# Token mixer, attention and thirty feed-forward passes: who adds 0.01 tanh, and who adds the variance's constant

## The chip, the cores and the metric

The kernel runs on one core of one Trainium2 chip. The metric is the time of one execution on the device in microseconds. The kernel before has a median of 1579.58 us over three runs (1578.74 to 1583.05).

## The reference

Frames of 75 joints go through three graph layers and a mean (the tokens), text is appended, one attention layer is added, and then a feed-forward part. The change lies in that last part, which goes thirty times over a matrix `x` of 64 x 96 rows of 64 numbers:

```
def step(h, _):
    h = h + 0.01 * jnp.tanh(h)
    h = h * jax.nn.sigmoid(h)
    h = _layernorm(h, ln_w, ln_b)      # (h - mean) * rsqrt(var + 1e-5) * ln_w + ln_b
    h = jnp.einsum('bsc,dc->bsd', h, W) + b
    return (h, None)
x, _ = jax.lax.scan(step, layernorm(h), None, length=30)
out = h + x
```

## The kernel before

The last stage (`feed_forward`, from L1178) cuts the 6144 rows into six chunks. A chunk is a tile of 128 partitions x 512 numbers, eight rows of 64 on a partition. Each chunk owns one bank of PSUM (`ps[:, c]`), in which its `x` stays for all thirty passes; two more banks take the transposes.

A *step* is one chunk of one pass: 180 steps. All engines go through the steps in the same order (`steps`, L1225), each as an in-order queue, and are held together by semaphores alone. The first twelve steps are written out, then a loop of 28 turns with six steps in each, then five closing steps. In step `s` the engines work on chunks of different age: tanh and the addition on step `s`, silu and statistics on `s-1`, the scaling and the transposes on `s-3`, the copy of the transposed tile on `s-4`, the matrix on `s-5`. A chunk thus comes back to its own bank six steps later.

For one chunk the work is:

- ScalarE: `th = tanh(x)` (L1313).
- the addition `x + 0.01 th` in PSUM: TensorE for even chunks, as a product of `th` with a diagonal matrix `pct` that is accumulated into the bank (L1345), VectorE for odd chunks (L1402). In the opening pass VectorE does all six, in SBUF (L1398). Two semaphores `y_ready` count the two kinds; the waiting side counts halves (`half(lag)`).
- ScalarE: `g = silu(.)` from PSUM to SBUF (L1323).
- VectorE: four `bn_stats`, each over a pair of rows interleaved, which leave mean and summed squares of the deviations (64 times the variance) of every row (L1360); then, behind a wait for its own statistics, the sum of that and `D * EPS` into `var` (L1363).
- GpSimd: `rs = var ** -0.5` as a two-input power, 128 x 8 (L1296).
- VectorE: the scaling `gn = g * rs` (L1409). The mean isn't subtracted here: the weights were centred beforehand.
- TensorE transposes four 128 x 128 squares (L1353), ScalarE copies them to SBUF (L1330), TensorE writes the bias into the bank and accumulates the matrix (L1338, L1340).

VectorE's order within a step is: addition (if it is its turn), scaling of `s-3`, statistics of `s-1`. So the scaling of one chunk comes two steps after its statistics, with one scaling and one set of statistics between. `var`, `rs`, the pairs of the statistics and `gn` have two buffers each. GpSimd's power of step `n` waits for `var` of `n` and for the scaling of `n-2`.

Of the kernel before, what the change touches and what calls it, by code (L numbers as in the profile page):

```python
# [22 lines left out]
ALU = mybir.AluOpType  # L23
# [4 lines left out]
P = 128  # L28
# [3 lines left out]
D = 64  # L32
# [1145 lines left out]
def feed_forward(nc, ctx, ps, h2, h2_loaded, ident, wf, pct, ones, brow, out):  # L1178
# [8 lines left out]
    def sb(name, shape, dt=F32):  # L1187
        return ctx.enter_context(nc.sbuf_tensor(name, shape, dt))
# [11 lines left out]
    var, var0 = (sb(f"var64_{i}", [P, n, CR]) for i, n in enumerate((2, CH)))  # L1200
    rs, rs0 = (sb(f"rs_{i}", [P, n, CR]) for i, n in enumerate((2, CH)))
    expo = sb("expo", [P, CR])
    warm = sb("warm", [P, 1])

    bn0 = sem("bn_done0")
# [19 lines left out]
    def steps(eng, body, before=None):  # L1225

        for s in range(2 * CH):
            if before and s < CH:
                before(s)
            body(s, s % CH, lambda lag, s=s: s - lag >= 0, lambda lag, s=s: (s - lag) // 2 - CH // 2)  # L1230
        with eng.Fori(1, ITERS - 1) as it:
            for c in range(CH):
                body(it * CH + CH + c, c, lambda lag: True, lambda lag, c=c: it * (CH // 2) + (c - lag) // 2)
        for s in range(N, N + LAG):
            body(s, s - N, lambda lag, s=s: 0 <= s - lag < N, lambda lag, s=s: (s - lag) // 2 - CH // 2)

    def opening(n):

        return isinstance(n, int) and n < CH
# [5 lines left out]
    def squares(pairs, b):  # L1245
        return pairs[:, b].rearrange("p j (i k) -> p (j i) k", i=2)[:, :, 2]
# [28 lines left out]
    def prepare_pool(pool, t):  # L1275

        if t == 10:
            pool.memset(expo[:], -0.5).then_inc(expo_made, 1)
            pool.wait_ge(expo_made, 1)
        if t in STATS_AT:  # L1280
            pool_root(pool, STATS_AT.index(t))
        if t in CENTRE_AT:
            pool_centre(pool, CENTRE_AT.index(t))

    def gpsimd(pool):
        def before(s):
            if s in LATE_STATS_AT:
                pool_root(pool, EARLY + LATE_STATS_AT.index(s))

        def body(s, c, on, half):  # L1290
            if on(1):
                n, b = s - 1, (c - 1) % 2
                pool.wait_ge(var_done, n + 1)
                if late(n, 2):
                    pool.wait_ge(gn_done, n - 1)
                nc.gpsimd.tensor_tensor(rs[:, b, :], var[:, b, :], expo[:], ALU.pow).then_inc(rs_done, 1)  # L1296
        steps(pool, body, before)

    def scalar(act):

        nc.scalar.activation(warm[:], ident[:, 0:1], ACT.Silu)

        def body(s, c, on, half):
            if on(0):
                if opening(s):
                    act.wait_ge(x0_ready, s + 1)
                else:
                    act.wait_ge(x_ready, s - CH + 1)
                if late(s, CH + 2):
                    act.wait_ge(y_ready[c % 2], half(2) + 1)  # L1310
                elif late(s, 2):
                    act.wait_ge(y0_made, s - 1)
                nc.scalar.activation(th[:, c % 2, :], x0[:, c, :] if opening(s) else ps[:, c, :],  # L1313
                                     ACT.Tanh).then_inc(th_done, 1)
            if on(1):
                n, cn = s - 1, (c - 1) % CH
                if opening(n):
                    act.wait_ge(y0_made, n + 1)
                else:
                    act.wait_ge(y_ready[cn % 2], half(1) + 1)  # L1320
                if late(n, NG):
                    act.wait_ge(gn_done, n - NG + 1)
                nc.scalar.activation(g_[:, cn % NG].rearrange("p r d -> p (r d)"), x0[:, cn, :] if opening(n) else ps[:, cn, :],  # L1323
                                     ACT.Silu).then_inc(g_done, 1)
            if on(4):
                n, b = s - 4, c % 2
                act.wait_ge(gT_ready, n + 1)
                if late(n, 2):
                    act.wait_ge(x_ready, n - 1)
                nc.scalar.activation(gT[:, b, :], ps[:, TB + b, :], ACT.Identity).then_inc(gT_done, 1)  # L1330
        steps(act, body)

    def tensor(pe):
        def body(s, c, on, half):
            if on(5):
                n, cn, b = s - 5, (c - 5) % CH, (c - 5) % 2
                pe.wait_ge(gT_done, n + 1)
                nc.tensor.matmul(ps[:, cn, :], ones[:], brow[:], start=True, stop=False, skip_group_check=True)  # L1338
                for j in range(CP):
                    last = nc.tensor.matmul(ps[:, cn, j * P:(j + 1) * P], gT[:, b, j * P:(j + 1) * P], wf,  # L1340
                                            start=False, stop=(j == CP - 1), skip_group_check=True)
                last.then_inc(x_ready, 1)
            if on(0) and c % 2 == 0 and not opening(s):
                pe.wait_ge(th_done, s + 1)
                nc.tensor.matmul(ps[:, c, :], pct[:], th[:, c % 2, :], start=False, stop=True,  # L1345
                                 skip_group_check=True).then_inc(y_ready[0], 1)
            if on(3):
                n, b = s - 3, (c - 3) % 2
                pe.wait_ge(gn_done, n + 1)
                if late(n, 2):  # L1350
                    pe.wait_ge(gT_done, n - 1)
                for j in range(CP):
                    last = nc.tensor.transpose(ps[:, TB + b, j * P:(j + 1) * P], gn[:, b, j, :], ident[:])  # L1353
                last.then_inc(gT_ready, 1)
        steps(pe, body)

    def statistics(dve, src, pairs, var, b, n, bns, made):

        for j in range(CP):
            last = v_.bn_stats(pairs[:, b, j, :], src[:, 2 * j:2 * j + 2, :].rearrange("p i d -> p d i"))  # L1360
        last.then_inc(bns, 1)
        dve.wait_ge(bns, n + 1)
        v_.tensor_scalar(var[:, b, :], squares(pairs, b), D * EPS, None, ALU.add).then_inc(made, 1)  # L1363

    def first_statistics(dve, c):
        dve.wait_ge(h2_loaded, (c + 1) * 16)
        statistics(dve, rows(c), bs0, var0, c, c, bn0, var0_done)

    def first_scale(dve, c):
        x = x0[:, c, :].rearrange("p (r d) -> p r d", d=D)  # L1370
# [12 lines left out]
    def vector(dve):  # L1383
        def before(s):
            if s in LATE_STATS_AT:
                c = EARLY + LATE_STATS_AT.index(s)
                first_statistics(dve, c)
                v_.tensor_tensor(x0[:, c, :].rearrange("p (r d) -> p r d", d=D), rows(c),
                                 spread(means(bs0, c), P, CR), ALU.subtract).then_inc(centred[1], 1)
            if s in LATE_SCALE_AT:  # L1390
                c = EARLY + LATE_SCALE_AT.index(s)
                dve.wait_ge(centred[1], c - EARLY + 1)
                first_scale(dve, c)

        def body(s, c, on, half):
            if on(0) and opening(s):
                dve.wait_ge(th_done, s + 1)
                v_.scalar_tensor_tensor(x0[:, c, :], th[:, c % 2, :], 0.01, x0[:, c, :],  # L1398
                                        ALU.mult, ALU.add).then_inc(y0_made, 1)
            elif on(0) and c % 2 == 1:  # L1400
                dve.wait_ge(th_done, s + 1)
                v_.scalar_tensor_tensor(ps[:, c, :], th[:, c % 2, :], 0.01, ps[:, c, :],  # L1402
                                        ALU.mult, ALU.add).then_inc(y_ready[1], 1)
            if on(3):
                n, cn, b = s - 3, (c - 3) % CH, (c - 3) % 2
                dve.wait_ge(rs_done, n + 1)
                if late(n, 2):
                    dve.wait_ge(gT_ready, n - 1)
                v_.tensor_tensor(gn[:, b].rearrange("p j (i d) -> p (j i) d", i=2), g_[:, cn % NG],  # L1409
                                 spread(rs[:, b, :], P, CR), ALU.mult).then_inc(gn_done, 1)  # L1410
            if on(1):
                n, cn, b = s - 1, (c - 1) % CH, (c - 1) % 2
                dve.wait_ge(g_done, n + 1)
                if late(n, 2):
                    dve.wait_ge(rs_done, n - 1)
                statistics(dve, g_[:, cn % NG], bs, var, b, n, bn_done, var_done)
        steps(dve, body, before)
        for c in range(CH):
            dve.wait_ge(x_ready, N - CH + c + 1)
            v_.tensor_tensor(h2[:, c, :], h2[:, c, :], ps[:, c, :], ALU.add).then_inc(out_done, 1)  # L1420
# [45 lines left out]
```

## Time and profile before

| | |
|---|---|
| median of three runs | 1579.58 us |
| the profiled execution's own time | 1579.94 us |
| its span, first to last instruction | 1578.1 us |
| TensorE (PE) busy | 1505.3 us, 95% |
| VectorE (DVE) busy | 1368.2 us, 87% |
| GpSimd (POOL) busy | 1240.5 us, 79% |
| ScalarE (ACT) busy | 1154.8 us, 73% |

These shares are means over the whole span. The tokens take the first 1100 us or so, the attention about the next 100, and the last stage runs from 1208 us to the end. To judge a change in that stage one reads stretches of it, a turn of the loop for instance, and the order of single instructions in the timeline. An instruction that an engine holds in its queue for a semaphore isn't busy time; one that has started and can't get its data is.

### The profile page before, as it was taken

The numbers are of one execution on the slowest core, as the hardware profiler recorded it, in microseconds if no ns is written. First come the engines' busy times: TensorE is split into PE (matmuls) and PEld (weight loads), VectorE is DVE, ScalarE is ACT, GpSimd is POOL, SyncE is SP. The second block draws the span as 40 slices with busy tenths as digits, with TensorE's granted clock in tenths as the row PEclk, the third lists the DMA queues.
The fourth block names the chain that finished last, engine by engine and source line by source line (L and its number), as shares of the span: only waits on it lengthen the run. The fifth ranks groups of instructions, "written<-read, shape, count | busy, mean of one in ns | idle before, by whom it ended". The sixth has DMA issues, their size and how long they took to land. (4 is left out here: it accounts for less than half of the span.)

```text
span 1578.1 us, 64590 instructions
## 1 busy us (share of the span) xinstructions
PE 1505.3 (95%) x22398; PEld 1162.8 (74%) x22398; DVE 1368.2 (87%) x3354; ACT 1154.8 (73%) x2706; POOL 1240.5 (79%) x1295
## 2 busy tenths in 40 slices
PE   8599999999999999999999999999495999999998
PEld 8477777777777777777777777776484888888887
DVE  7388888888888888888888888888578999999998
ACT  3477787777777777778777777776054888787876
POOL 2288888888888888888888888888167888888887
PEclk9999999999999999999999999999696999999999
DMA  5300000000000000000000000000111000000001
GB/s 116 100 9 7 7 7 7 7 7 7 7 7 7 7 7 7 7 7 7 7 7 7 7 7 7 7 7 6 19 46 36 1 0 0 0 0 0 0 0 40
DMA packets 21670, 21.66 MB, mean 14 GB/s; under 512 B 12254, under 2 KB 19342, under 8 KB 21271
## 3 DMA queue, kind: packets, MB, share of 16 engines
q1 hardware_dynamic: 18554, 19.07, 4.5%
q0 software_dynamic: 1120, 1.44, 0.4%
q10 hardware_dynamic: 1972, 0.86, 0.3%
q8 instruction: 13, 0.21, 0.1%
q14 instruction: 11, 0.09, 0.0%
HBM read 14.43 MB, written 6.92 MB: 14 GB/s over the span
## 5 line engine op out<-in xcount | busy, mean ns | idle before, releaser
L703 DVE SCALAR_TENSOR_TENSOR y<-ps,negb,abar 128x375 f32<-128x375 f32 x820 | 459.4, 602 | 95.2 <-PE ps L603 95.1
L657 POOL TENSOR_TENSOR y0lo<-y_whole,y0hi 128x384 f16<-128x384 f32 x410 | 375.1, 915 | 165.5 <-ACT y_whole L631 152.3
L581 PE MATMUL ps<-AThi,y0hi 64*128 64x150 f16 (+1 forms) x4920 | 434.6, 217 | 3.4 <-POOL y0lo L657 3.4
L581 PE MATMUL ps<-AThi,y0lo 64*128 64x150 f16 (+1 forms) x4920 | 435.2, 215 | 0.0
L581 PE MATMUL ps<-ATlo,y0hi 64*128 64x150 f16 (+1 forms) x4920 | 434.9, 214 | 0.0
L666 POOL TENSOR_TENSOR y<-y 128x370 f32<-128x370 f32 x410 | 399.0, 973 | 2.0 <-DVE y L703 1.9
L629 ACT ACTIVATE y0hi<-ps 128x384 f16<-128x384 f32 x410 | 202.7, 494 | 234.4 <-POOL y0lo L657 220.5
L1296 POOL TENSOR_TENSOR rs<-var,expo 128x8 f32<-128x8 f32 x180 | 313.8, 1753 | 49.7 <-DVE var L1363 49.7
L603 PE MATMUL ps<-z_whole,W1s 128*128 128x375 f32 x820 | 313.7, 504 | 0.0
L638 ACT ACTIVATE z_whole<-ps 128x375 f32<-128x375 f32 x615 | 268.8, 493 | 1.4 <-PE ps L581 1.4
L581 PEld LDWEIGHTS ps<-ATlo,y0hi 64*128 64x128 f16 x4920 | 244.2, 96 | 0.0
L581 PEld LDWEIGHTS ps<-AThi,y0hi 64*128 64x128 f16 x4920 | 239.3, 94 | 4.3 <-POOL y0lo L657 3.7
L691 DVE SCALAR_TENSOR_TENSOR y0lo<-ps,y0hi 128x384 f16<-128x384 f32 x410 | 226.6, 553 | 18.0 <-ACT y0hi L629 17.6
L581 PEld LDWEIGHTS ps<-AThi,y0lo 64*128 64x128 f16 x4920 | 238.7, 94 | 0.0
L631 ACT ACTIVATE y_whole<-ps 128x384 f32<-128x384 f32 x410 | 209.7, 511 | 0.0
L630 ACT ACTIVATE y0hi<-ps 128x384 f16<-128x384 f32 x410 | 204.4, 498 | 0.0
L1340 PEld LDWEIGHTS ps<-w,gT 128*128 128x128 f32 x1440 | 189.9, 192 | 7.6
L603 PEld LDWEIGHTS ps<-z_whole,W1s 128*128 128x128 f32 x820 | 139.2, 189 | 73.1
L1340 PE MATMUL ps<-w,gT 128*128 128x128 f32 x1440 | 190.5, 275 | 0.0
L715 DVE TENSOR_REDUCE pooledT<-y 128x190 f32 (+3 forms) x410 | 182.5, 446 | 0.7 <-POOL y L666 0.7
L560 PEld LDWEIGHTS ps<-W0K,z_static 64*128 64x128 f16 x2460 | 73.6, 95 | 123.3 <-issue 119.5
L597 PE MATMUL ps<-z_whole,W1s 128*128 128x375 f32 x410 | 162.6, 478 | 0.0
(201 smaller groups left out, 2366.2 us busy)
## 6 DMA issues: line engine op xcount, KB each, us to landing
z_static<-z_rows SPq DMA_DIRECT2D x410, 18.0 KB
xs<-in_x_v SPq DMA_DIRECT2D x5, 720.7 KB, 8.6
z_rows<-zp SPq DMA_DIRECT2D x10, 240.0 KB
h_rows<-h SPq DMA_DIRECT2D x16, 96.0 KB, 1.9
h2r<-h_rows SPq DMA_DIRECT2D x6, 256.0 KB, 2.6
out<-h2r SPq DMA_DIRECT2D x6, 256.0 KB, 2.3
z_rows<-zp POOLq DMA_DIRECT2D x5, 240.0 KB, 3.0
h<-in_txt SPq DMA_DIRECT2D x1, 512.0 KB, 5.0
```

What stands on the lines that cost most here:

```text
L581: last = nc.tensor.matmul(ps[:, Z1B + 2 * p + j, f0 * V:f0 * V + w], y[rows, par, p, t * C:(t + 1) * C], a[rows, BAND0[t]:BAND0[t] + w], s ...
L603: nc.tensor.matmul(ps[:, Y1B[1][i], 0:GV], W1s[:], z1f[:, par, 1 + i, :], start=True, stop=True).then_inc(y1_ready[i], 1)
L629: nc.scalar.activation(y0hi[:, par, p, HC:2 * HC], ps[:, Y0B + 1, 0:HC], ACT.Relu).then_inc(y0hi_done, 1)
L630: nc.scalar.activation(y0hi[:, par, p, 0:HC], ps[:, Y0B, 0:HC], ACT.Relu).then_inc(y0hi_done, 1)
L631: nc.scalar.activation(y0f[:, p, :], ps[:, Y0B, 0:HC], ACT.Relu).then_inc(y0f_done, 1)
L638: nc.scalar.activation(z1f[:, par, 2 * p + i - 1, :], ps[:, Z1B + 2 * p + i, 0:GV], ACT.Identity).then_inc(z1f_done, 1)
L657: nc.gpsimd.tensor_tensor(y0lo[:, par, p, 0:HC], y0f[:, p, :], y0hi[:, par, p, 0:HC], ALU.subtract).then_inc(y0lo_by_pool, 1)
L666: nc.gpsimd.tensor_tensor(y[:, :, U1:2 * U1], y[:, :, U1:2 * U1], y[:, :, 0:U1], ALU.add).then_inc(halved, 1)
L691: nc.vector.scalar_tensor_tensor(y0lo[:, par, p, HC:2 * HC], ps[:, Y0B + 1, 0:HC], 0.0, y0hi[:, par, p, HC:2 * HC], ALU.max, ALU.subtract) ...
L703: nc.vector.scalar_tensor_tensor(y1[:, par, 2 * p + i].rearrange("p f v -> p (f v)"), ps[:, Y1B[p][i], 0:GV], negb1[:, 0:1], abar[:].rearr ...
L1296: nc.gpsimd.tensor_tensor(rs[:, b, :], var[:, b, :], expo[:], ALU.pow).then_inc(rs_done, 1)
L1340: last = nc.tensor.matmul(ps[:, cn, j * P:(j + 1) * P], gT[:, b, j * P:(j + 1) * P], wf, start=False, stop=(j == CP - 1), skip_group_check ...
```

## The change

TensorE adds 0.01 tanh in chunks 0 and 3 and VectorE in the other four (before: 0, 2, 4 and 1, 3, 5). The two counts of `y_ready` follow that; waits take a pair (pass, chunk) and not a half. The instruction L1363 on VectorE, with its wait, goes from the loop. In its place GpSimd adds a tile `eps64` that holds `D * EPS` to the statistics, two inputs of 128 x 8, into `var`. It waits for the statistics and for the power of the step before, and the power waits for this addition. The statistics ahead of the loop keep their instruction on VectorE.

```
+    eps64 = sb("eps64", [P, CR])
...
+    def added_by_tensor(c):
+        return c % 3 == 0
+
+    def wait_added(eng, place):
+        k, c = place
+        if added_by_tensor(c):
+            eng.wait_ge(y_ready[0], k * (CH // 3) + c // 3 + 1)
+        else:
+            eng.wait_ge(y_ready[1], k * (CH - CH // 3) + c - c // 3)
...
         if t == 10:
+            pool.memset(eps64[:], D * EPS)
...
                 n, b = s - 1, (c - 1) % 2
+                pool.wait_ge(bn_done, n + 1)
+                if late(n, 1):
+                    pool.wait_ge(rs_done, n)
+                nc.gpsimd.tensor_tensor(var[:, b, :], squares(bs, b), eps64[:], ALU.add).then_inc(var_done, 1)
                 pool.wait_ge(var_done, n + 1)
...
-                    act.wait_ge(y_ready[c % 2], half(2) + 1)
+                    wait_added(act, place(2))
...
-            if on(0) and c % 2 == 0 and not opening(s):
+            if on(0) and added_by_tensor(c) and not opening(s):
...
-        last.then_inc(bns, 1)
-        dve.wait_ge(bns, n + 1)
-        v_.tensor_scalar(var[:, b, :], squares(pairs, b), D * EPS, None, ALU.add).then_inc(made, 1)
+        last.then_inc(made, 1)
...
-            elif on(0) and c % 2 == 1:
+            elif on(0) and not added_by_tensor(c):
...
-                statistics(dve, g_[:, cn % NG], bs, var, b, n, bn_done, var_done)
+                statistics(g_[:, cn % NG], bs, b, bn_done)
```

## Rows read from the trace of the kernel before

**Rows 1.** Stretches: from:to, length, busy us (instructions) of each engine, TensorE's clock, DMA
```profile
1398.84:1410.85 12.01, 12.01 (x86) 10.00 (x85) 11.42 (x39) 9.62 (x19) 10.42 (x6) 1.00 0.00 0
...
1170.00:1180.00 10.00, 8.23 (x86) 7.50 (x84) 7.60 (x23) 5.06 (x15) 8.09 (x10) 1.00 0.28 76
```

**Rows 2.** Groups, whole run: line, operation, shapes, count | busy us, mean ns | idle before, releaser
```profile
L666 POOL TENSOR_TENSOR y<-y 128x370 f32<-128x370 f32 x410 | 399.0, 973 | 2.0 <-DVE y L703 1.9
...
L1296 POOL TENSOR_TENSOR rs<-var,expo 128x8 f32<-128x8 f32 x180 | 313.8, 1753 | 49.7 <-DVE var L1363 49.7
...
L1360 DVE BATCH_NORM_STATS2 bn_pairs<-g 128x6 f32<-128x128 f32 x720 | 158.1, 282 | 0.6 <-ACT g L1323 0.6
...
L1409 DVE TENSOR_TENSOR gn<-g,rs 128x512 f32<-128x512 f32 x180 | 123.9, 688 | 12.1 <-issue 10.4 <-POOL rs L1296 1.4
...
L669 POOL TENSOR_TENSOR y<-y 128x190 f32<-128x190 f32 x205 | 109.0, 532 | 16.1
...
L1048 POOL TENSOR_TENSOR hn<-hc,rstd 96x256 f32<-96x256 f32 x16 | 9.7, 609 | 9.4 <-PE ps L1104 8.0 <-POOL hc L1043 0.8
...
L1272 POOL TENSOR_TENSOR x<-h2r,bn_pairs 128x512 f32<-128x512 f32 x4 | 4.2, 1049 | 0.0
```

**Rows 3.** Chain that ended last, 1400 to 1410: start us, length us, what
```profile
1403.91 0.86 PE ps L1345 x2
...
1404.77 0.44 PE ps L1353 x4
...
1405.20 0.22 PE ps L1338
...
1405.42 0.89 PE ps L1340 x8
```

**Rows 4.** Timeline, 1400 to 1413: start us, length us, engine, line, operation [idle before]
```profile
1400.80 0.70 DVE L1402 SCALAR_TENSOR_TENSOR ps<-th,ps 128x512 f32<-128x512 f32 x1
...
1401.03 1.64 POOL L1296 TENSOR_TENSOR rs<-var,expo 128x8 f32<-128x8 f32 x1 [0.52 <-DVE var L1363]
...
1401.40 0.69 DVE L1409 TENSOR_TENSOR gn<-g,rs 128x512 f32<-128x512 f32 x1
...
1402.01 0.88 DVE L1360 BATCH_NORM_STATS2 bn_pairs<-g 128x6 f32<-128x128 f32 x4
...
1402.92 0.17 DVE L1363 TENSOR_SCALAR var<-bn_pairs 128x8 f32<-128x8 f32 x1
...
1403.00 0.69 DVE L1409 TENSOR_TENSOR gn<-g,rs 128x512 f32<-128x512 f32 x1
...
1405.22 0.69 DVE L1409 TENSOR_TENSOR gn<-g,rs 128x512 f32<-128x512 f32 x1
...
1406.82 0.69 DVE L1409 TENSOR_TENSOR gn<-g,rs 128x512 f32<-128x512 f32 x1
...
1411.19 0.69 DVE L1409 TENSOR_TENSOR gn<-g,rs 128x512 f32<-128x512 f32 x1 [0.38 <-issue]
```

**Rows 5.** Timeline of GpSimd alone, three short windows behind 1403
```profile
1403.25 1.94 POOL L1296 TENSOR_TENSOR rs<-var,expo 128x8 f32<-128x8 f32 x1 [0.58 <-DVE var L1363]
...
1403.25 3.54 POOL L1296 TENSOR_TENSOR rs<-var,expo 128x8 f32<-128x8 f32 x2 [0.58 <-DVE var L1363]
...
1406.99 2.01 POOL L1296 TENSOR_TENSOR rs<-var,expo 128x8 f32<-128x8 f32 x1 [0.21 <-DVE var L1363]
```

**Rows 6.** Timeline of GpSimd in the attention
```profile
1169.11 0.10 POOL L1278 MEMSET expo<- 128x8 f32 x1
...
1184.01 0.61 POOL L1043 TENSOR_TENSOR hc<-h,mean 96x256 f32<-96x256 f32 x1
...
1184.70 0.61 POOL L1048 TENSOR_TENSOR hn<-hc,rstd 96x256 f32<-96x256 f32 x1
```

More of the change, by code:

```diff
@@ L1229, in steps @@
                 before(s)
-            body(s, s % CH, lambda lag, s=s: s - lag >= 0, lambda lag, s=s: (s - lag) // 2 - CH // 2)
+            body(s, s % CH, lambda lag, s=s: s - lag >= 0, lambda lag, s=s: ((s - lag) // CH - 1, (s - lag) % CH))
         with eng.Fori(1, ITERS - 1) as it:
             for c in range(CH):
-                body(it * CH + CH + c, c, lambda lag: True, lambda lag, c=c: it * (CH // 2) + (c - lag) // 2)
+                body(it * CH + CH + c, c, lambda lag: True, lambda lag, c=c: (it + (c - lag) // CH, (c - lag) % CH))
         for s in range(N, N + LAG):
-            body(s, s - N, lambda lag, s=s: 0 <= s - lag < N, lambda lag, s=s: (s - lag) // 2 - CH // 2)
+            body(s, s - N, lambda lag, s=s: 0 <= s - lag < N, lambda lag, s=s: ((s - lag) // CH - 1, (s - lag) % CH))
+    def added_by_tensor(c):
[6 more added lines that the diff above has]
+            eng.wait_ge(y_ready[1], k * (CH - CH // 3) + c - c // 3)
     def opening(n):
@@ L1288, in before, with body @@
                 pool_root(pool, EARLY + LATE_STATS_AT.index(s))
-        def body(s, c, on, half):
+        def body(s, c, on, place):
             if on(1):
                 n, b = s - 1, (c - 1) % 2
+                pool.wait_ge(bn_done, n + 1)
+                if late(n, 1):
+                    pool.wait_ge(rs_done, n)
+                nc.gpsimd.tensor_tensor(var[:, b, :], squares(bs, b), eps64[:], ALU.add).then_inc(var_done, 1)
                 pool.wait_ge(var_done, n + 1)
@@ L1301, in scalar, with body @@
         nc.scalar.activation(warm[:], ident[:, 0:1], ACT.Silu)
-        def body(s, c, on, half):
+        def body(s, c, on, place):
             if on(0):
@@ L1319, in body @@
                 else:
-                    act.wait_ge(y_ready[cn % 2], half(1) + 1)
+                    wait_added(act, place(1))
                 if late(n, NG):
@@ L1333, in tensor, with body @@
     def tensor(pe):
-        def body(s, c, on, half):
+        def body(s, c, on, place):
             if on(5):
@@ L1355, in tensor, with statistics @@
         steps(pe, body)
-    def statistics(dve, src, pairs, var, b, n, bns, made):
+    def statistics(src, pairs, b, made):
         for j in range(CP):
             last = v_.bn_stats(pairs[:, b, j, :], src[:, 2 * j:2 * j + 2, :].rearrange("p i d -> p d i"))
-        last.then_inc(bns, 1)
-        dve.wait_ge(bns, n + 1)
-        v_.tensor_scalar(var[:, b, :], squares(pairs, b), D * EPS, None, ALU.add).then_inc(made, 1)
+        last.then_inc(made, 1)
     def first_statistics(dve, c):
         dve.wait_ge(h2_loaded, (c + 1) * 16)
-        statistics(dve, rows(c), bs0, var0, c, c, bn0, var0_done)
+        statistics(rows(c), bs0, c, bn0)
+        dve.wait_ge(bn0, c + 1)
+        v_.tensor_scalar(var0[:, c, :], squares(bs0, c), D * EPS, None, ALU.add).then_inc(var0_done, 1)
     def first_scale(dve, c):
@@ L1393, in before, with body @@
                 first_scale(dve, c)
-        def body(s, c, on, half):
+        def body(s, c, on, place):
             if on(0) and opening(s):
```

## The prediction

> **What bounds the kernel now.** I read the stretches of the last stage first. In one turn of its loop TensorE is busy all 12.01 us, VectorE 11.42, GpSimd 10.42, ScalarE 9.62, at a granted clock of 1.00 [rows 1]. Three engines within 13% of each other: cutting one only helps until the next one limits, so each needs its own bill by step. A turn has six steps, one per chunk, so a step lasts 2.00 us; 180 powers [rows 2] make 180 steps, of which the first six are the opening pass, and 174 (29 turns) go by the loop's pace, 348 us of the run.
>
> TensorE's bill is in the chain of waits, which is TensorE alone here: the matrix 0.89, the bias 0.22, the transposes 0.44, and in every second step 0.86 for adding 0.01 tanh [rows 3]. That is 1.55 and 2.41 us, 11.88 a turn.
>
> VectorE's is read from starts in the timeline [rows 4]. Scaling to the next statistics: 1401.40 to 1402.01, 0.61. Statistics to the variance instruction (L1363): 0.91. That one to the next scaling: 0.08. So 1.60 without an addition of its own; with one (1403.00 to 1405.22) 2.22. Three of each are 11.46, and the turn of the loop holds the scaling at 1411.19 another 0.38: 11.84. TensorE and VectorE are equally the bound.
>
> GpSimd has one power a step and stands 49.7 us in all for the variance ahead of it [rows 2]. The power's mean is 1753 ns, but that mean hides two kinds. The one at 1401.03 took 1.64 [rows 4], the ones at 1403.25 and 1406.99 took 1.94 and 2.01 [rows 5]. The long ones start while L1409's scaling runs: it ran 1403.00 to 1403.69, and the power ended at 1405.19, 1.50 later; it ran 1406.82 to 1407.51, and the power ended at 1409.00, 1.49 later. A power that starts inside a scaling gets nowhere until the scaling is over, and then needs 1.49. The power at 1401.03 started inside VectorE's addition (1400.80 to 1401.50) and lost nothing. The scaling reads two SBUF tiles (gn<-g,rs), the addition one SBUF tile and PSUM.
>
> The Trainium skill says in "GPSIMD Engine Reference", section 1, Specifications, that GpSimd's SBUF interfaces are shared with VectorE, with contention against VectorE instructions that have two SBUF inputs. The trace agrees, with 1.94 and 2.01 us under the scaling against 1.64 under the addition. By that rule the added instruction, which reads SBUF as well, can be held just like the power; by the undisturbed rows alone the sum would be rival 2's.
>
> **The change, part by part.**
>
> *TensorE adds in two chunks of six, not three.* Two steps of 2.41 and four of 1.55: 11.02 a turn, 0.86 less.
>
> *VectorE adds in four, and loses L1363.* Four statistics instructions take 0.88 together and 0.28 each [rows 2, 4], so they start 0.20 apart, and the instruction behind the last overlaps it by 0.08 as one behind a scaling does (0.69 long, 0.61 to the next). From the statistics on it is then 0.80 instead of 0.91 + 0.08. An addition takes 0.60 to the next start (1400.80 to 1401.40). So 1.41 without and 2.01 with: 2 x 1.41 + 4 x 2.01 + 0.38 = 11.24 a turn, against 11.84.
>
> *GpSimd adds the constant ahead of each power, between two waits.* The added waits are for its own instructions: the addition waits for the power before it, the power for the addition. Queued behind them on GpSimd is only the next such pair; the scaling on VectorE waits for the power. What a wait for an own instruction costs is seen in the attention: the multiply at 1184.70 waits for the subtraction that ended at 1184.62, 0.08 [rows 6]. A wait with register work ahead of it takes longer: L1363 ended at 1403.09, the power started at 1403.25, 0.16 [rows 4, 5]. No row shows an addition of 128x8. From below, the memset of 128x8 took 0.10 [rows 6], and the line through the operations on 190 and 370 elements (532 and 973 ns) gives 0.09 for eight [rows 2]; from above, the line from the 256-element one (0.61) to the 512-element one (1049 ns) leaves 0.18 [rows 2]. I take 0.12, near the memset of the same shape. Undisturbed, GpSimd then needs 0.08 + 0.12 + 0.08 + 1.64 = 1.92 a step, 11.52 a turn: more than VectorE's 11.24 and TensorE's 11.02. So GpSimd becomes the bound, and that is what starts the trouble. The constant's memset, once, costs 0.10 and is hidden in the attention.
>
> *What is late next.* When GpSimd is the slowest, VectorE stands at L1409 and waits for the power. Its scaling starts at the soonest 0.03 to 0.04 after the power's end: the power at 1403.25 ended at 1405.19 and the scaling that needs it began at 1405.22; the next ended at 1406.79, its scaling began at 1406.82 [rows 4, 5]. The next addition on GpSimd waits for the same power and starts 0.08 after it, thus 0.04 into the scaling, and is held for the length of it. In each step the end of one power releases the scaling that blocks the next pair. One step is then: 0.04 to the scaling, 0.69 of it, the addition done about when it ends (a held power had 1.49 of 1.64 left, 0.15 less, and the addition is no longer than that; at most 0.03 behind), 0.08, and the power 1.64, for which no second scaling comes: 2.45 us. VectorE's longest way from one scaling to the next, 2.01, and TensorE's 2.41 in two steps of six and 1.55 in the others fit inside, so nothing else waits for long.
>
> Bounds: if the addition reads before the scaling starts and only the power is held, the scaling has to start 0.07 behind the addition's start (the second power of the pair at 1403.25 began about there, ahead of the scaling at 1405.22, and was not held), and the step is 0.08 + 0.07 + 0.69 + 1.49 = 2.33. If the addition takes 0.18 and the second wait 0.16, it is 2.56. I take 2.45 for five steps of six and 2.33 for the one where VectorE comes late from the turn of the loop: 14.58 a turn against 12.01, 2.57 x 29 = 74.5 us.
>
> *Opening pass.* Six steps in which VectorE's own additions read two SBUF tiles too; a hold of some 0.3 each, 2 us.
>
> **Sum.** 1579.94 us for the profiled execution (span 1578.1, 1.8 around it; 0.4 above the median shown) + 74.5 + 2 = 1656 us.
>
> **The rivals.**
>
> 1. *The addition slips past, only the power is held.* 2.33 in all steps: 13.98 a turn, 1.97 x 29 = 57, plus 2: 1639. For it: 0.04 us decides, and register work ahead of the scaling's wait would delay it by as much. Against it: the two scalings at 0.03 behind their powers.
>
> 2. *Nothing is held, faster.* If the scaling starts after the power has begun to read (0.08 + 0.12 + 0.08 and a little, some 0.35 behind the power before), the step is GpSimd's 1.92: 0.49 x 29 = 14 less, 1566; with a free addition VectorE's 11.24, 22 less, 1558. The point that decides is the length of the hold: a step is 2.00 now, so beside the power's 1.64 there is room for 0.36, of which waits and addition take 0.28; a hold above 0.08 a step makes the change slower. For it: four of the six powers in a turn now run undisturbed, because their start falls outside a scaling. Against it: they do so because GpSimd waits for VectorE; with the order turned round, the scaling follows the power's end.
>
> 3. *TensorE's clock falls.* TensorE would work 11.02 of 14.58 us, 76%. In the attention it was busy 8.23 of 10 us at a granted clock of 1.00 [rows 1]. If it fell to 1.2 GHz for half of the time, its 11.02 us would be 16.5 a turn: 4.5 x 29 = 131 more, 1711; all the time 22.0, 1870. For it: no row of a busy share near 76% at the full clock. Against it: the waits are short and come in every step.
>
> 4. *No change.* The split brings what it should and a hold in one or two steps of six takes it back: 1575 to 1585.
>
> **How the numbers follow.** Forecast 0.55, with 1640 to 1685 as its own range (2.56 in all steps is 15.36 a turn, 3.35 x 29 + 2 = 99, 1679, and some microseconds for the opening; below it lies rival 1's time). Rival 1 0.17, rival 2 0.12, rival 3 0.07, rival 4 0.04, and 0.05 for holds in some steps only, 1585 to 1630. A measurement of this kernel tells 0.3% (5 us) from no change. Slower is the forecast, rivals 1 and 3 and the partial holds: 0.84; same 0.04; faster 0.12. The range 1605 to 1695 leaves out rivals 2, 3 and 4 and a part of the 0.05, some 2 in 10 with the forecast's own tail above.
>
> **What would show it.** In the profile after: the turn of the loop at 14 to 15 us; VectorE's L1409 waiting for GpSimd's power in nearly every step, where now it hardly does; GpSimd's busy share near all of it, with the added instruction at 0.5 to 0.8 us where held and 0.1 where not, or the power near 2.0 to 2.2 where the addition slipped by; TensorE's busy share down by a fifth or more, with its idle time ended by the scaling. Wrong would be: L1409 not waiting, powers at 1.64 and the step under 2.0 (then the hold is not what lengthened the powers, or does not follow the release); the hold there but the step well under 2.3 (then an interrupted instruction keeps more of its work than 0.15).

## The result, and the profile after

The changed kernel takes 1662.4 us (median of six runs, 1661.7 to 1670.3), the kernel before 1581.9 in the runs beside it: a ratio of 1.0524, 95% interval 1.05 to 1.0548. The quotient of the two medians is 1.051; the ratios of the experiments can differ from theirs by as little too. Every run had a mean granted clock of 0.981 to 0.987 but one of e5's four, which took 1745.9 us at 0.846 and does not count in e5's time. The changed kernel is slower by 80 us, and the time lies in the last stage: one turn of its loop, the same six steps, now lasts 14.92 us. The stretch of one turn after, in the columns of [rows 1]:

```profile
1399.98:1414.90 14.92, 12.14 (x83) 9.62 (x82) 11.32 (x35) 10.25 (x18) 13.57 (x12) 1.00 0.00 0
```

TensorE and VectorE no longer fill the turn; GpSimd is busy 13.57 of 14.92 us, and the clock is still 1.00. The chain that ended last, TensorE's before [rows 3], is now GpSimd's (part 4 of the profile's page: shares of the span by engine, then by line; the chain goes back to about 1140 us, the last 32% of the span):

```profile
POOL 25%; PE 3%; issue 2%; DVE 1%; POOLq 1%; ACT 0%; DVEq 0%
POOL rs L1314 18%; POOL var L1310 6%; PE ps L1092 1%; PE ps L1064 1%; PE ps L1074 0%; PE ps L1096 0%; PE ps L1083 0%; POOL rs L1281 0%; POOLq L1307 0%; DVE h2r L1438 0%; PE ps L1104 0%; POOLq L1313 0%; DVE bn_pairs L1378 0%; POOLq L1309 0%; DVE x L1390 0%
```

The groups of the last stage after, 1240 to 1665, in the columns of [rows 2]. L1310 is the new addition, L1314 the power, L1427 the scaling (before: none, L1296, L1409):

```profile
L1314 POOL TENSOR_TENSOR rs<-var,expo 128x8 f32<-128x8 f32 x170 | 285.3, 1678 | 15.6 <-POOL var L1310 4.4
...
L1427 DVE TENSOR_TENSOR gn<-g,rs 128x512 f32<-128x512 f32 x170 | 118.0, 694 | 103.7 <-POOL rs L1314 99.9
...
L1310 POOL TENSOR_TENSOR var<-bn_pairs,eps 128x8 f32<-128x8 f32 x169 | 98.7, 584 | 22.4
```

The scaling stood 1.4 us for the power in the whole run before [rows 2]; it now stands 99.9 us in this stage. The power has become shorter in the mean (1753 to 1678 ns) and the addition of eight numbers costs 584. Why, the timeline of GpSimd and VectorE tells (start, length, and in brackets the wait):

```profile
1399.98 0.69 DVE L1427 TENSOR_TENSOR gn<-g,rs 128x512 f32<-128x512 f32 x1 [0.42 <-POOL rs L1314]
1400.09 0.64 POOL L1310 TENSOR_TENSOR var<-bn_pairs,eps 128x8 f32<-128x8 f32 x1
...
1400.81 1.64 POOL L1314 TENSOR_TENSOR rs<-var,expo 128x8 f32<-128x8 f32 x1
...
1402.57 0.69 DVE L1427 TENSOR_TENSOR gn<-g,rs 128x512 f32<-128x512 f32 x1 [1.11 <-POOL rs L1314]
1402.59 0.73 POOL L1310 TENSOR_TENSOR var<-bn_pairs,eps 128x8 f32<-128x8 f32 x1
...
1403.40 1.64 POOL L1314 TENSOR_TENSOR rs<-var,expo 128x8 f32<-128x8 f32 x1
...
1405.12 0.20 POOL L1310 TENSOR_TENSOR var<-bn_pairs,eps 128x8 f32<-128x8 f32 x1
1405.16 0.71 DVE L1427 TENSOR_TENSOR gn<-g,rs 128x512 f32<-128x512 f32 x1 [0.51 <-POOL rs L1314]
1405.48 1.88 POOL L1314 TENSOR_TENSOR rs<-var,expo 128x8 f32<-128x8 f32 x1 [0.16 <-POOL var L1310]
...
1407.40 0.69 DVE L1427 TENSOR_TENSOR gn<-g,rs 128x512 f32<-128x512 f32 x1
1407.51 0.64 POOL L1310 TENSOR_TENSOR var<-bn_pairs,eps 128x8 f32<-128x8 f32 x1
```

The scaling at 1399.98 runs to 1400.67. The addition starts 0.11 into it and ends at 1400.73, 0.06 behind it, whether it started 0.11 into it (0.64 long) or 0.02 (0.73 long, at 1402.59). The power then runs its 1.64, its end at 1402.45 releases the next scaling at 1402.57 and the next addition at 1402.59, and the scaling has won again. Once in a turn, at 1405.12, the addition starts 0.04 ahead of the scaling: it takes 0.20, and the power, at 1405.48 inside the scaling, is held in its place and ends at 1407.36, 1.49 behind the scaling's end (1405.87), as the prediction read it from [rows 4] and [rows 5]. Two things meet there: the scaling starts 0.12 behind the power and not 0.03, and the addition 0.08 behind it and not 0.14. At 1402.57 the scaling is as late, but the addition comes 0.14 behind the power and is held.

The steps from scaling to scaling are 2.59, 2.59, 2.24, 2.50, 2.50 and 2.50 from 1399.98 on, 14.92 in all. Counted from one power's end to the next they are 2.50, 2.59, 2.32, 2.51, 2.50 and 2.50. The profiled execution took 1670.3 us, one of the two longest of the six. Its 90 us over the one profiled before are 2.91 x 29 = 84 in the loop's pace, 1.6 in the opening pass (from the first scaling to the seventh 15.09 us, before 13.51), and 4.1 by which the first scaling came later, behind tokens and attention in which the change adds one memset.

### The profile page after: what moved, and what is told of

The parts are those of the page before. It is cut to its first block and busy times, and to the rows that moved or that the text cites. A ratio compares the mean times of both kernels' runs of the same rounds, so it can differ in the third digit from the quotient of the medians.

```text
span 1668.4 us, 64767 instructions
## 1 busy us (share of the span) xinstructions
PE 1510.7 (91%) x22340; PEld 1151.1 (69%) x22340; DVE 1364.3 (82%) x3203; ACT 1172.2 (70%) x2706; POOL 1335.7 (80%) x1476
## 5 line engine op out<-in xcount | busy, mean ns | idle before, releaser
L1314 POOL TENSOR_TENSOR rs<-var,expo 128x8 f32<-128x8 f32 x180 | 301.6, 1676 | 16.3 <-POOL var L1310 4.4
L603 PE MATMUL ps<-z_whole,W1s 128*128 128x375 f32 x820 | 313.7, 504 | 0.0
L1427 DVE TENSOR_TENSOR gn<-g,rs 128x512 f32<-128x512 f32 x180 | 124.9, 694 | 108.9 <-POOL rs L1314 105.0
L1371 PE MATMUL ps<-ident,gn 128*128 128x128 f32 x720 | 119.2, 289 | 96.8 <-DVE gn L1427 96.8
L1371 PEld LDWEIGHTS ps<-ident,gn 128*128 128x128 f32 x720 | 76.5, 142 | 163.3 <-DVE gn L1427 162.8
```

Of the source, the lines that this page charges most:

```text
L603: nc.tensor.matmul(ps[:, Y1B[1][i], 0:GV], W1s[:], z1f[:, par, 1 + i, :], start=True, stop=True).then_inc(y1_ready[i], 1)
```

## The experiments

The kernel before had 1578.3 us beside the first four and 1580.0 beside the others; all diffs are against the changed kernel.

**e1: the same kernel, with a scaling that has one SBUF input.**

```
-  v_.tensor_tensor(gn[...], g_[:, cn % NG],
+  v_.tensor_tensor(gn[...], g_[:, cn % NG] if opening(n) else ps[:, cn, :],   # rearranged to p r d
```

> The changed kernel, but VectorE's scaling reads the chunk in PSUM (its silu is left out) and not the SBUF tile g, so that it has one SBUF input. Theory (a scaling with two SBUF inputs holds GpSimd): every addition 0.20 us, every power 1.64, a step of GpSimd's own 0.14 + 0.20 + 0.08 + 1.64 = 2.06 us, the run at about 1592 us. Rival A (the added instruction and its waits are that long by themselves): additions still 0.64, step 2.49, 1662 us. Rival B (VectorE's additional PSUM work delays the stage): 1650 us or more, VectorE busy all the time.

Measured: 1593.2 us, ratio 1.0089 (1.0073 to 1.0106). Groups (1240 to 1575) and timeline:

```profile
L1314 POOL TENSOR_TENSOR rs<-var,expo 128x8 f32<-128x8 f32 x164 | 268.4, 1636 | 15.1 <-POOL var L1310 4.4
L1427 DVE TENSOR_TENSOR gn<-ps,rs 128x512 f32<-128x512 f32 x163 | 112.7, 691 | 33.6 <-POOL rs L1314 33.6
L1310 POOL TENSOR_TENSOR var<-bn_pairs,eps 128x8 f32<-128x8 f32 x163 | 33.1, 203 | 21.6
```

```profile
1401.54 1.64 POOL L1314 TENSOR_TENSOR rs<-var,expo 128x8 f32<-128x8 f32 x1
1403.21 0.69 DVE L1427 TENSOR_TENSOR gn<-ps,rs 128x512 f32<-128x512 f32 x1 [0.58 <-POOL rs L1314]
1403.32 0.20 POOL L1310 TENSOR_TENSOR var<-bn_pairs,eps 128x8 f32<-128x8 f32 x1
```

The order is the same: the power ends at 1403.18, the scaling starts at 1403.21, the addition at 1403.32, 0.11 into it. The scaling is as long as in the changed kernel (691 against 694 ns). But now the addition takes 0.20, in the mean 203 ns instead of 584, the power 1636 in the mean, and the loss against the kernel before is 15 us in place of 80. So the hold is a matter of the scaling's second SBUF input, and neither the added instruction's own length nor the release is the bulk of the loss. The run has its own counterpart: in the opening pass its scaling still reads `g` from SBUF, and there the addition is held as in the changed kernel:

```profile
1219.84 0.69 DVE L1427 TENSOR_TENSOR gn<-g,rs 128x512 f32<-128x512 f32 x1 [0.42 <-POOL rs L1314]
1219.95 0.64 POOL L1310 TENSOR_TENSOR var<-bn_pairs,eps 128x8 f32<-128x8 f32 x1
```

The first six steps take 15.09 us in e1, a turn of its loop 12.38. The loop also gives GpSimd's pace without any hold: 0.14 + 0.20 + 0.08 + 1.64 = 2.06, still above the 2.00 of before. The power is all that VectorE waits for there (33.6 us), so this pace is GpSimd's; the ring of e2 below has nearly the same turn, 12.35, but with waits for tanh. The Trainium skill ("GPSIMD Engine Reference", section 1, Specifications) names two SBUF inputs of the VectorE instruction as a condition of the contention; this pair of runs agrees, 584 ns with two and 203 with one.

**e4: the addition released early.**

```
-                if late(n, 1):
-                    pool.wait_ge(rs_done, n)
+                if late(n, 2):
+                    pool.wait_ge(rs_done, n - 1)
```

> The changed kernel, but the addition waits for the power before last, whose input it overwrites, and not for the last one; it then starts right behind the last power, ahead of the scaling. Theory (hold): additions 0.20 us, the power is held in their place and ends 1.49 behind the scaling: step 2.21 to 2.30, powers 1.85 to 2.1, 1618 to 1634 us. Rival A (length of its own): additions still 0.64, only the wait of 0.14 saved, step 2.35, 1638 us, powers 1.64. Rival C (the waits between own instructions are the cost): one wait of two less, and the step near 2.1, 1600 us.

Measured: 1622.3 us, ratio 1.0277 (1.026 to 1.0294). Groups (same stretch) and timeline:

```profile
L1314 POOL TENSOR_TENSOR rs<-var,expo 128x8 f32<-128x8 f32 x150 | 300.7, 2005 | 11.8
...
L1310 POOL TENSOR_TENSOR var<-bn_pairs,eps 128x8 f32<-128x8 f32 x149 | 29.5, 198 | 0.0
```

```profile
1402.10 0.20 POOL L1310 TENSOR_TENSOR var<-bn_pairs,eps 128x8 f32<-128x8 f32 x1
1402.16 0.69 DVE L1427 TENSOR_TENSOR gn<-g,rs 128x512 f32<-128x512 f32 x1 [0.74 <-POOL rs L1314]
1402.38 1.98 POOL L1314 TENSOR_TENSOR rs<-var,expo 128x8 f32<-128x8 f32 x1
```

The addition starts 0.06 ahead of the scaling (0.15 in two steps of six), is free of it (198 ns in the mean), and the power takes the hold: 2005 ns in the mean. The power above ends at 1404.36, 1.51 behind the scaling's end at 1402.85. The hold moves from one instruction to the other as the theory says. Four steps of a turn last 2.22 us, two 2.31.

**e3: only GpSimd's addition, with every second chunk as before.**

```
-        return c % 3 == 0
+        return c % 2 == 0        # and both counts of y_ready in halves
```

> Only GpSimd's addition: TensorE and VectorE keep every second chunk each, as in the kernel before, and VectorE has lost L1363. Theory: GpSimd sets the pace in the same cycle, 2.45 to 2.5 us a step, 1655 to 1665 us. Rival B (the split delays the stage): near TensorE's 11.88 us a turn, 1575 to 1582 us.

Measured: 1665.2 us, ratio 1.0551 (1.0533 to 1.057). VectorE's waits, 1240 to 1540 (engine, line, for whom: us in total, times, longest):

```profile
DVE gn L1427 <- POOL rs L1314: 84.2, 121, 1.1
```

The loss is all there without the split, in the same pattern of steps: a turn is 14.91 us, with the addition held in five steps of six.

**e2: no addition, with the split by thirds.**

```
-                if late(n, 1):
-                    pool.wait_ge(rs_done, n)
-                nc.gpsimd.tensor_tensor(var[:, b, :], squares(bs, b), eps64[:], ALU.add).then_inc(var_done, 1)
-                pool.wait_ge(var_done, n + 1)
...
-                nc.gpsimd.tensor_tensor(rs[:, b, :], var[:, b, :], expo[:], ALU.pow).then_inc(rs_done, 1)
+                nc.gpsimd.tensor_tensor(rs[:, b, :], squares(bs, b), expo[:], ALU.pow).then_inc(rs_done, 1)
```

> The changed kernel without the added instruction: the power reads the statistics themselves, and D * EPS is left out in the loop. Theory: what costs is the added instruction alone; the new split and the missing variance instruction on VectorE are worth what the bills said, VectorE 11.24 to 11.4 us a turn, so 1560 to 1567 us, powers mostly 1.64. Rival B (the split delays the stage): 1582 us or more. Rival A says the same as the theory here.

Measured: 1590.0 us, ratio 1.007 (1.0053 to 1.0086). This missed the expectation by 23 us or more: with GpSimd's addition gone the split still makes the kernel slower. One turn, the waits of VectorE (1240 to 1580), and three steps of the timeline:

```profile
1399.43:1411.78 12.35, 11.41 (x84) 9.72 (x83) 11.10 (x35) 9.78 (x19) 10.49 (x7) 1.00 0.00 0
```

```profile
DVE ps L1416 <- ACT th L1327: 34.2, 110, 0.3
```

```profile
1405.61 0.68 DVE L1423 TENSOR_TENSOR gn<-g,rs 128x512 f32<-128x512 f32 x1
...
1406.35 0.65 PE L1367 MATMUL ps<-ident,gn 128*128 128x128 f32 x4 [0.47 <-DVE gn L1423]
...
1407.05 1.05 PE L1354 MATMUL ps<-w,gT 128*128 128x128 f32 x8
...
1407.94 1.02 PE L1359 MATMUL ps<-th,pct 128*128 128x512 f32 x2
...
1408.81 0.60 PE L1367 MATMUL ps<-ident,gn 128*128 128x128 f32 x4
...
1409.46 1.05 PE L1354 MATMUL ps<-w,gT 128*128 128x128 f32 x8
...
1410.55 0.60 ACT L1327 ACTIVATE th<-ps 128x512 f32<-128x512 f32 x1 [0.46 <-PE ps L1354]
...
1411.18 0.70 DVE L1416 SCALAR_TENSOR_TENSOR ps<-th,ps 128x512 f32<-128x512 f32 x1 [0.32 <-ACT th L1327]
...
1411.78 0.69 DVE L1423 TENSOR_TENSOR gn<-g,rs 128x512 f32<-128x512 f32 x1
```

VectorE's busy time, 11.10, is near its bill of 11.24; but four times a turn its addition waits 0.31 for tanh, and 11.10 + 1.24 is the turn of 12.35 but for 0.01. The rows show a ring. The scaling at 1405.61 lets TensorE transpose at 1406.35; TensorE then goes without a pause through a matrix, its own addition, the transposes and the next matrix; tanh follows at 1410.55, the addition at 1411.18, the scaling at 1411.78: 6.17 us for three steps, 12.34 a turn. This is theory D of the next runs.

**e6: the ring cut.** Here the diff is against e2:

```
-  nc.scalar.activation(th[...], x0[:, c, :] if opening(s) else ps[:, c, :],
+  nc.scalar.activation(th[...], x0[:, c, :] if opening(s) or not added_by_tensor(c) else ps[:, c, :],
...
-                dve.wait_ge(th_done, s + 1)
-                v_.scalar_tensor_tensor(ps[:, c, :], th[:, c % 2, :], 0.01, ps[:, c, :],
+                dve.wait_ge(x_ready, s - CH + 1)
+                v_.scalar_tensor_tensor(ps[:, c, :], x0[:, c, :], 0.01, ps[:, c, :],
```

> The run without the constant, and VectorE's addition in the loop adds a tile in SBUF that is ready (x0) in place of tanh and waits for the matrix alone; ScalarE's tanh of those chunks reads that tile too, so that nothing writes under it. Left out: D * EPS and the true tanh of four chunks in six. Theory D: the ring is 0.6 us shorter per three steps, below VectorE's own 11.24 to 11.4 a turn, so 1560 to 1567 us. Rival F (the power is held by the scaling in two steps of six and that delays VectorE): 1590 as in the run without the constant, since nothing on GpSimd changes.

Measured: 1557.5 us, ratio 0.9861 (0.9838 to 0.9884), just below the expected span. One turn:

```profile
1366.28:1377.56 11.28, 11.18 (x82) 9.74 (x83) 11.00 (x35) 9.70 (x19) 10.50 (x7) 1.00 0.00 0
```

With the wait for tanh gone VectorE has no wait left in this stretch and the turn is 11.28, near the 11.24 of the bill. Powers are held in two steps of six here too and cost nothing, so rival F falls. One of them is among these three, which take 5.24 and not 3 x 1.64 = 4.92:

```profile
1369.83 5.24 POOL L1310 TENSOR_TENSOR rs<-bn_pairs,expo 128x8 f32<-128x8 f32 x3 [0.27 <-DVE bn_pairs L1374]
```

**e5: only the split.**

```
-                pool.wait_ge(bn_done, n + 1)
-                if late(n, 1):
-                    pool.wait_ge(rs_done, n)
-                nc.gpsimd.tensor_tensor(var[:, b, :], squares(bs, b), eps64[:], ALU.add).then_inc(var_done, 1)
...
                 statistics(g_[:, cn % NG], bs, b, bn_done)
+                dve.wait_ge(bn_done, n + 1)
+                v_.tensor_scalar(var[:, b, :], squares(bs, b), D * EPS, None, ALU.add).then_inc(var_done, 1)
```

> Only the split by thirds; the variance instruction stays on VectorE and GpSimd has nothing added. VectorE's bill by the rows of before is 6 x 1.60 + 4 x 0.62 + 0.38 = 12.46 us a turn against 12.01. Theory D (with thirds a ring closes: VectorE's addition waits for tanh, tanh for the matrix, the matrix in TensorE's queue behind the transposes, those for the scaling that follows the addition; 6.17 us for three steps in the run without the constant): VectorE's own work is longer than that ring, so 12.46, some 1591 us, hardly any wait for tanh. Rival E (the addition has to wait for tanh about 0.3 us four times a turn whatever else VectorE does): 13.7 a turn, 1627 us.

Measured: 1597.5 us, ratio 1.0108 (1.008 to 1.0137). VectorE does not wait for tanh at all, as D says; its only entry in the list of waits is the turn of the loop:

```profile
DVE gn L1423 <- issue: 9.3, 24, 0.4
```

So rival E, with 1627, falls. The time is some 6 us above the 1591 of the bill, and they lie in the loop. One turn:

```profile
1394.91:1407.60 12.69, 11.53 (x82) 9.75 (x84) 12.03 (x40) 9.82 (x18) 10.16 (x7) 1.00 0.00 0
```

That is 0.23 above the bill's 12.46. Of it 0.09 is an error of the bill, which also sits in the prediction's 11.84: it lets the 0.38 at the turn of the loop begin 0.08 behind the start of the variance instruction, where the next instruction elsewhere starts, but this is idle time and begins at that instruction's end, 0.17 behind its start. The other 0.14 is one addition that starts 0.24 behind the start of the variance instruction (1404.69 to 1404.93), elsewhere 0.10; why is open.

**e7: halves, no constant.** The edits of e3 and e2 together:

```
-        return c % 3 == 0
+        return c % 2 == 0
...
-                nc.gpsimd.tensor_tensor(var[:, b, :], squares(bs, b), eps64[:], ALU.add).then_inc(var_done, 1)
...
+                nc.gpsimd.tensor_tensor(rs[:, b, :], squares(bs, b), expo[:], ALU.pow).then_inc(rs_done, 1)
```

> TensorE and VectorE keep every second chunk as before, and the constant is left out (the power reads the statistics; D * EPS is missing in the loop). VectorE 11.84 - 6 x 0.19 = 10.7 us a turn, TensorE 11.88. Theory D: TensorE is the bound, the ring closes over two steps and is shorter: 1574 to 1579 us. Rival F: held powers delay it beyond the kernel before, over 1582.

Measured: 1575.1 us, ratio 0.997 (0.9959 to 0.9981). A turn is 11.84 us, TensorE's bill of 11.88. So taking L1363 from VectorE, and its work from everyone, is worth 0.3% while TensorE has every second chunk.

**e8: halves, the constant on ScalarE.** The edit of e3, no addition on GpSimd, and in ScalarE's body behind tanh:

```
+            if on(2):
+                n, b = s - 2, c % 2
+                act.wait_ge(bn_done, n + 1)
+                if late(n, 2):
+                    act.wait_ge(rs_done, n - 1)
+                nc.scalar.activation(var[:, b, :], squares(bs, b), ACT.Identity, bias=eps64[:, 0:1]).then_inc(var_done, 1)
```

> TensorE and VectorE keep every second chunk, and ScalarE adds the constant (an activation with a bias, behind tanh of the second step after), so neither VectorE nor GpSimd has it; the reference in full. If the 0.2 to 0.3 us by which the power starts later stay hidden: TensorE's bound, 1574 to 1580 us. If they reach the scaling in the steps where it began 0.03 us behind its power: 1585 to 1600 us.

Measured: 1578.7 us, ratio 0.9986 (0.9973 to 1.0): within the first expectation, and not told from the kernel before. Of the changed kernels that compute the whole reference it is the fastest here, and no gain that these runs can show.

## Why the prediction was right, and where it was not

*The cycle* was right, step by step: GpSimd becomes the bound, VectorE's scaling waits for the power, the power's end releases the scaling ahead of the next addition, the addition is held until the scaling ends, and the power runs free. e1 and e4 show the hold itself, e3 that the split has no part in it. The step, which the forecast counts from one power's end to the next, was put at 2.45 in five steps and 2.33 in one; it is 2.50 or 2.51 in four, 2.59 in one and 2.32 in one. The 2.59 has a scaling that starts 0.12 behind the power and not 0.03, with the addition held all the same. The 2.32 has a scaling as late, and the addition slips past because it also starts sooner, 0.08 behind the power. In e1, where nothing of the loop is held, the addition starts 0.07 to 0.08 behind the power once a turn too, so this is no effect of the hold; what it comes from is not shown.

*The terms.* The addition takes 0.20 undisturbed (e1), where 0.12 was taken and 0.18 was the bound from above: the line through longer operations is no upper bound for a short one. The wait ahead of it costs 0.14 and not 0.08 in five steps of six. Both hardly touched the forecast, because the hold covers them. The addition ends 0.06 behind the scaling, where the forecast had it done about with the scaling, and the scaling starts 0.03 behind the power and not 0.04: a held step is 0.05 longer. One held step has its scaling 0.09 later, and the slipping step is 0.01 shorter: 5 x 0.05 + 0.09 - 0.01 = 0.33 a turn, nearly all of the 10 us between 74.5 and 84 in the profiled execution. They do touch rival 2. TensorE is busy 12.14 us a turn and not 11.02, so its share fell to 81% and by a little less than the fifth that was to show.

*The opening pass* cost 1.6 us, near the 2 of the forecast, but not by its reason. It put a hold of some 0.3 down to VectorE's own additions in SBUF. From the first scaling to the seventh the trace shows the loop's cycle already, one step of 2.59 and five of 2.50.

*Luck.* By the profiles the last stage lost 84 + 1.6 = 86 us, where 76.5 were forecast. That 1656 is only 6 us below the median of 1662 is in part luck: the first scaling came between 1208.9 (e5) and 1215.7 us (changed kernel) in the profiles, and the changed kernel's profiled execution was the latest of them.

*Rival 2* (nothing held, 1566 us) had the wrong price on both sides. Its 1.92 a step is 2.06, and e1, which is that rival made real, is slower than the kernel before. Its floor, the bill of 11.24 us for VectorE and 11.02 for TensorE, left out that the two are tied in a ring through tanh: e2 has nothing on GpSimd but the power and takes 1590 us. The step of the working that failed is "VectorE adds in four, and loses L1363": the busy time fell as worked out, and waits for tanh took it back. e6, where that wait is cut, is the only run that collects it, and it leaves out a part of the result.

*Rivals 1, 3 and 4.* The addition slipped past in one step of six, not in all; e4 is rival 1 made real, and takes 1622 where 1639 was worked out, since an addition released early is ahead of the scaling without the scaling having to come late. The clock stayed at 1.00 with TensorE busy 12.14 of 14.92 us. The split brought nothing that a hold could have taken back.

## What to carry to other kernels

When an engine off the critical path gets an instruction, add up its whole pace, own waits included, and ask whether it becomes the bound; from then on its end releases its consumer, and whatever the consumer holds up (here, by its second SBUF input, GpSimd) meets the next instruction in almost every step (five additions and one power in six steps), where before it met two powers in six. A bill of busy times per engine is a floor: before it counts as a gain, follow the ring of waits through the in-order queues once around, as e2 and e6 show (1590 and 1557.5 us). A mean duration that hides two kinds, 1.64 and 2.01, is the place to look first.

## What the runs showed of the hardware

- A GpSimd instruction that starts 0.02 or 0.11 us into a VectorE operation with two SBUF inputs ends 0.06 behind it if it is short (0.73 and 0.64 instead of 0.20); one that starts 0.04 or more ahead of it runs free (an addition 0.20 in e4 and the changed kernel; the power at 1401.03, 0.37 ahead of a scaling, 1.64 [rows 4]). With one input from PSUM nothing is held (203 ns in the mean, e1's loop).
- A power of 128x8 takes 1.64 us on GpSimd, an addition of the same shape 0.20.
- A VectorE instruction that waits for the result of the one ahead started later here than one that doesn't: L1363 0.91 behind the start of the statistics before [rows 4], the scaling without L1363 0.79 behind it (1400.03 to 1400.82 in e2).
